# Graph attention over sorted edges: V products of three tiles in sixteen on POOL, K times Q sums of two on ACT, and masked maxima in place of a second pair of scans

## What is computed

```python
q = (x @ Wq + bq).reshape(n, H, DK)      # H = 8, DK = 64
k = (x @ Wk + bk).reshape(n, H, DK)
v = (x @ Wv + bv).reshape(n, H, DK)
logits = jnp.einsum('ehd,ehd->eh', q[rows] * scale, k[cols]) + att_bias
row_max = jax.ops.segment_max(logits, rows, num_segments=n)
p = jnp.exp(logits - row_max[rows])
denom = jax.ops.segment_sum(p, rows, num_segments=n)
att = p / denom[rows]
y = jax.ops.segment_sum(att[:, :, None] * v[cols], rows, num_segments=n)
out = y.reshape(n, H * DK) @ Wo + bo
```

## Time and profile before

| | |
|---|---|
| median of 3 runs | 3250.69 us (3249.51 to 3252.86) |
| profiled execution, its own time | 3252.61 us |
| span of the profile | 3250.8 us |
| busy: PE, DVE, ACT, POOL | 2883.9, 2864.1, 2188.3, 2211.0 us |
| granted TensorE clock, mean over the span | 0.94 |
| HBM read, written | 550.28 MB, 61.49 MB |

### The profile page before, as it was taken

How to read it: one execution, slowest core, us unless ns; L and a number is a source line. 1 busy time by engine, 2 the same in 40 slices (tenths; PEclk the granted TensorE clock), 3 DMA queues, 4 the chain that set the end, 5 groups by cost and what they waited for, 6 DMA issues and landing times.

```text
span 3250.8 us, 62874 instructions
## 1 busy us (share of the span) xinstructions
PE 2883.9 (89%) x11814; PEld 1680.8 (52%) x11939; DVE 2864.1 (88%) x20476; ACT 2188.3 (67%) x7706; POOL 2211.0 (68%) x2512
## 2 busy tenths in 40 slices
PE   4899888888888278999999999999999999989998
PEld 3555554445555135555555555555555555554444
DVE  8997777777777378999999999999999999998887
ACT  8332222222222048999999999999999999974444
POOL 0477777777777756777878778777878787851121
PEclk6798899888888689999999999999999999999999
DMA  6343333333333487888888888888888888841222
GB/s 188 84 136 105 107 111 107 113 107 107 106 104 93 163 307 251 262 262 259 259 261 263 260 259 265 259 264 259 264 260 260 260 263 259 259 140 61 83 79 71
DMA packets 259303, 615.95 MB, mean 189 GB/s; under 512 B 69771, under 2 KB 80343, under 8 KB 258658
## 3 DMA queue, kind: packets, MB, share of 16 engines
q0 software_dynamic: 144832, 443.72, 43.5%
q1 hardware_dynamic: 110434, 160.86, 16.5%
q10 hardware_dynamic: 3648, 7.34, 0.6%
HBM read 550.28 MB, written 61.49 MB: 188 GB/s over the span
## 4 chain that ended last, share of the span: by engine, by line
DVE 46%; POOL 23%; issue 14%; PE 12%; DMA 2%; DVEq 1%; ACT 1%; SPq 0%; POOLq 0%
DVE big L1339 25%; POOL rec_scratch L667 23%; DVE big L1449 12%; PE banks L2000 5%; PE banks L2065 2%; DVE big L1057 1%; DVEq L1449 1%; PE banks L1926 1%; PE banks L1979 1%; DMA big<-q_scratch 1%; DVE big L1434 1%; PE banks L1988 1%; DVE small L1401 1%; DMA big<-kv_scratch,small 1%; PE banks L2068 1%
## 5 line engine op out<-in xcount | busy, mean ns | idle before, releaser
L863 ACT ACTIVATE big<-big,small 128x65 f32<-128x65 f32 x6564 | 1605.1, 344 | 4.8
L688 POOL DMA_INDIRECT big<-kv_scratch,small x832 | 844.2, 1015 | 346.4 <-DVE big L1339 182.6
L1339 DVE SCALAR_TENSOR_TENSOR big<-banks,big 128x64 f32<-128x64 f32 x6656 | 1027.5, 213 | 32.6 <-DMA big<-kv_scratch,small 17.5
L667 POOL DMA_INDIRECT rec_scratch<-big,small x782 | 773.3, 989 | 323.4 <-issue 237.7
L1926 PE MATMUL banks<-big,small 128*128 x1664 | 889.7, 616 | 73.2 <-DVE big L1339 56.5
L1979 PE MATMUL banks<-big,small 128*128 128x260 f32 x3328 | 882.2, 388 | 45.6 <-POOL small L696 21.4
L1979 PEld LDWEIGHTS banks<-big,small 128*128 128x128 f32 x3328 | 615.0, 190 | 452.9 <-issue 271.9
L1817 PE MATMUL banks<-big 128*128 128x512 f32 (+1 forms) x1176 | 604.1, 662 | 34.8 <-DVE big L1047 34.8
L1449 DVE SCALAR_TENSOR_TENSOR big<-big,loS,banks 128x520 f32 x832 | 618.6, 744 | 6.3 <-PE banks L1979 4.2
L696 POOL TENSOR_SCALAR small<-iotaF,small 128x128 f32<-128x128 f32 x832 | 527.2, 634 | 60.5 <-PE banks L1979 34.8
L1339 DVE DVE_READ_ACCUMULATOR big<-banks,big 128x1 f32 x6656 | 513.5, 77 | 0.1
(11 more groups left out here) (273 smaller groups left out, 2639.7 us busy)
## 6 DMA issues: line engine op xcount, KB each, us to landing
rowR<-lo_rows SPq DMA_DIRECT2D x97, 256.0 KB
big<-src_rows SPq DMA_DIRECT2D x97, 256.0 KB, 3.6
big<-in_x_dram SPq DMA_DIRECT2D x96, 256.0 KB, 4.0
big<-kv_scratch,small POOLq DMA_INDIRECT x832, 5.3
rec_scratch<-big,small POOLq DMA_INDIRECT x782
kv_scratch<-big SPq DMA_DIRECT2D x48, 260.0 KB
q_scratch<-big SPq DMA_DIRECT2D x48, 256.0 KB
kv_scratch<-big SPq DMA_DIRECT2D x48, 256.0 KB
```

What stands on the lines that cost most here:

```text
L667: e.indirect_dma_start(recd, bass.IndirectOffsetOnAxis(ap=ridx[:, c % 4, j:j + 1], axis=0), rec[:, 8 * c + j, :], None).then_inc(s_sc[c % ...
L688: e.indirect_dma_start(KV[:, vat(t):vat(t) + YW + D], None, KVd, bass.IndirectOffsetOnAxis(ap=recB[b_ % 4][:, t % 16, 9:10].bitcast(i32), ...
L863: ins = e.activation(heads(Vr(t), h, h + 1), heads(Vr(t), h, h + 1), ACT.Copy, scale=ph[:, h:h + 1])
L1339: ins = e.scalar_tensor_tensor(k_, QB[t % 2][:, 64 * h:64 * h + 64], 1.0, k_, ALU.mult, ALU.mult, accum_out=Lr[t // 16 % 2][:, t % 16, h:h ...
```

## The change

Three parts, all in the attention stage.

1. `on_pool`: in each block the tiles t with t modulo 16 in (3, 8, 13) have V multiplied by p on POOL (`pvp`, one TENSOR_TENSOR of 128x520 with p broadcast along 65) instead of by 8 instructions on ACT. `pvp(s - 21)` stands on POOL behind `one_hot` in step s, so in steps r = 8, 13 and 2.
2. `summed`: the tiles with t modulo 16 in (4, 10), except in the last blocks, have K times Q as one DVE TENSOR_TENSOR of 128x512 in the first half of the step, and the sums over 64 by 8 ACTIVATEs with an accumulated sum on ACT (`sums`), two steps later and ahead of that step's `pva`. `gather` and `lb` wait for these sums.
3. `first_max` and `last_max`: the second pair of scans becomes two SCALAR_TENSOR_TENSORs on the result of the first pair, max(D2, mask + carried value), with masks that mark the edges of the tile's first and of its last source. The flags' row grows from 128 to 384 values for this, their buffers move to half of `rowR`, and the rows for the one-hots are loaded by half blocks. `scale_parts` becomes one instruction, with one more ACTIVATE on ACT (`p_less`) to take off 1.

The diff, cut to what the text speaks of:

```diff
-        QW = ((0, 8), (8, 16), (16, 24), (24, 28), (28, 33), (33, 40), (40, 49))
+        QW = ((0, 8), (8, 16), (16, 24), (24, 27), (27, 33), (33, 40), (40, 49))
...
-        sfr = [lc(130, bf16) for _ in range(2)]
+        sfr = [rowR[:, 1, 384 * i:384 * i + 384] for i in range(2)]
...
+        summed = [t % 16 in (4, 10) and t < LAST - 16 for t in range(T)]
+        sum_at = [sum(summed[:t + 1]) for t in range(T)]
+        s_sum, sum_base = s_ab, 2 * NCH
+        on_pool = [t % 16 in (3, 8, 13) and t < LAST for t in range(T)]
+        pvp_at = [sum(on_pool[:t + 1]) for t in range(T)]
+        s_pvp, pvp_base = s_hist, NCH
...
                 q.wait_ge(s_rd, k + 1)
+                if k >= 0:
+                    q.wait_ge(s_sum, sum_base + sum_at[k])
                 q.wait_ge(s_yt, v + 1)
...
+            def pvp(t):
+
+                v = Vr(t).rearrange("p (h d) -> p h d", d=65)
+                q.wait_ge(s_kv[t % 8], 16 * (t // 8 + 1))
+                q.wait_ge(s_ex, t // 16 + 1)
+                e.tensor_tensor(v, v, pB[t // 16 % 2][:, t % 16, :].rearrange("p (h a) -> p h a", a=1).broadcast_to([128, 8, 65]), ALU.mult).then_inc(s_pvp, 1)
...
                 if s - DEL - 2 >= 0:
                     one_hot(s - DEL - 2)
+                if 0 <= s - DEL + 2 < T and on_pool[s - DEL + 2]:
+                    pvp(s - DEL + 2)
...
+            def sums(t):
+
+                q.wait_ge(s_rd, t + 1)
+                q.wait_ge(s_x2, t // 16 - 1)
+                for h in range(8):
+                    k_ = Kr(t)[:, 64 * h:64 * h + 64]
+                    ins = e.activation(k_, k_, ACT.Copy, accum_out=Lr[t // 16 % 2][:, t % 16, h:h + 1])
+                ins.then_inc(s_sum, 1)
...
-                if s >= DEL:
+                if 2 <= s < T + 2 and summed[s - 2]:
+                    sums(s - 2)
+                if s >= DEL and not on_pool[s - DEL]:
                     pva(s - DEL)
                 if r_ == 5 and 0 <= b_ < NB:
                     p_fac(b_)
+                    p_less(b_)
                 if r_ == 6 and 0 <= b_ < NB:
                     p_exp(b_)
...
+                if summed[t]:
+                    if not half:
+                        e.tensor_tensor(Kr(t), QB[t % 2], Kr(t), ALU.mult).then_inc(s_rd, 1)
+                    return
                 for h in range(4 * half, 4 * half + 4):
...
-            def fwd2(b_):
+            def first_max(b_):
 
                 q.wait_ge(s_car, 2 * b_ + 2)
-                e.tensor_tensor_scan(F2, sfr[b_ % 2][:, 0:128], XP, Car[:, 1:2], ALU.add, ALU.max).then_inc(s_f2, 1)
-
-            def back2(b_):
+                q.wait_ge(s_d1, b_ + 1)
+                e.scalar_tensor_tensor(D2[b_ % 2], sfr[b_ % 2][:, 128:256], Car[:, 1:2], D2[b_ % 2], ALU.add, ALU.max).then_inc(s_f2, 1)
+
+            def last_max(b_):
 
                 q.wait_ge(s_f2, b_ + 1)
-                q.wait_ge(s_dt, b_ - 1)
-                e.tensor_tensor_scan(D2[b_ % 2][:, ::-1], sfr[b_ % 2][:, 1:129][:, ::-1], F2[:, ::-1], Car[:, 0:1], ALU.add, ALU.max).then_inc(s_m2, 1)
+                e.scalar_tensor_tensor(D2[b_ % 2], sfr[b_ % 2][:, 256:384], Car[:, 0:1], D2[b_ % 2], ALU.add, ALU.max).then_inc(s_m2, 1)
...
-                e.tensor_tensor(Aoh[0:8, :], iotaF[0:8, :], llb[0:8, max(b_ - 1, 0):max(b_ - 1, 0) + 1].broadcast_to([8, 128]), ALU.is_equal).then_inc(s_bd, 1)
-                e.scalar_tensor_tensor(Bd[0:8, :], ident[0:8, 0:8], fac[0:8, 0:1], nI[0:8, :], ALU.mult, ALU.add).then_inc(s_bd, 1)
+                e.scalar_tensor_tensor(Aoh[0:8, :], iotaF[0:8, :], llb[0:8, max(b_ - 1, 0):max(b_ - 1, 0) + 1], fac[0:8, 0:1].broadcast_to([8, 128]),
+                                       ALU.is_equal, ALU.mult).then_inc(s_bd, 1)
```

More of the change, by code:

```diff
@@ L549, in _ @@
             q.wait_ge(s_c5, 3)
-            rows5(0)
-            rows5(1)
-            q.wait_ge(s_idb, 3)
+            rows5(2)
+            rows5(3)
+            q.wait_ge(s_c5, 2)
             flags(0)
@@ L578, in _ @@
                     recs(b_)
-                q.wait_ge(s_rm, 4 * b_ - 4)
-                rows5(b_)
+                if b_ >= 5:
+                    q.wait_ge(s_ya, 16 * (b_ - 4))
+                    keeps(b_ - 1)
+                q.wait_ge(s_rm, 4 * b_ - 2)
+                rows5(2 * b_)
                 if b_ == 2:
@@ L851, in p_fac, with p_less @@
                 q.wait_ge(s_dd, b_ + 1)
-                q.wait_ge(s_bd, 2 * b_)
+                q.wait_ge(s_bd, b_)
                 e.activation(fac[0:8, 0:1], fac[0:8, 1:2], ACT.Exp, scale=-1.0).then_inc(s_fac, 1)
+            def p_less(b_):
+                q.wait_ge(s_fac, 2 * b_ + 1)
+                e.activation(fac[0:8, 0:1], fac[0:8, 0:1], ACT.Copy, bias=-1.0).then_inc(s_fac, 1)
+            def sums(t):
[5 more added lines that the diff above has]
+                ins.then_inc(s_sum, 1)
             def heads(v, h0, h1_):
@@ L1309, in one_hot_rows @@
                 e.memset(sfb[0:n, c, 0:1], 1.0).then_inc(s_v, 1)
-                nv += 2
+                for m in range(2):
+                    e.tensor_tensor(sfb[0:n, c, 128 + 128 * m:256 + 128 * m], lo_, ends2[0:n, c, m:m + 1].broadcast_to([n, 128]), ALU.is_equal).then_inc(s_v, 1)
+                nv += 4
                 e.tensor_tensor(rows3[0:n, c, 2, :], sqf[c % 2][0:n, :], rows3[0:n, c, 1, :], ALU.subtract).then_inc(s_v, 1)
@@ L1325, in _ @@
             first_oh(1)
-            for k in range(2):
-                e.memset(sfr[k][:, 128:129], 0.0).then_inc(s_idb, 1)
             win = wins(e, "dw")
@@ L1535, in _ @@
                 if at == 4:
-                    fwd2(b_)
+                    first_max(b_)
                 if at == 6:
@@ L1553, in _ @@
                 if at == 4:
-                    back2(b_)
+                    last_max(b_)
                 if s < T:
@@ L1932, in rows_oh @@
                 q.wait_ge(s_oh, k)
-                q.wait_ge(s_r[b_ % 2], 16 * (b_ // 2 + 1))
+                h = k // 2
+                q.wait_ge(s_r[h % 2], 16 * (h // 2))
                 q.wait_ge(s_c5, 3)
-                e.matmul(OHB, coef[:, :], row5[:, b_ % 2, 512 * (k % 4):512 * (k % 4) + 512], start=True, stop=True).then_inc(s_rm, 1)
+                e.matmul(OHB, coef[:, :], row5[:, h % 2, 512 * (k % 2):512 * (k % 2) + 512], start=True, stop=True).then_inc(s_rm, 1)
             def x2(b_):
@@ L1964, in scale1 @@
             def scale1(b_):
-                q.wait_ge(s_bd, 2 * b_ + 2)
+                q.wait_ge(s_bd, b_ + 1)
                 q.wait_ge(s_ex, b_ + 1)
                 q.wait_ge(s_sca, b_ - 1)
-                e.matmul(S1, Aoh[0:8, :], Bd[0:8, :], start=True, stop=True).then_inc(s_s1, 1)
+                e.matmul(S1, Aoh[0:8, :], ident[0:8, 0:8], start=True, stop=True).then_inc(s_s1, 1)
             def yt(t):
-                q.wait_ge(s_pva, t + 1)
+                q.wait_ge(s_pva, t + 1 - pvp_at[t])
                 q.wait_ge(s_pvv, t - LAST + 1)
+                if pvp_at[t]:
+                    q.wait_ge(s_pvp, pvp_base + pvp_at[t])
                 q.wait_ge(s_oh2, t + 1)
```

44 lines of the change are left out of this document (23 added, 21 removed).

## The result

The kernel with the change takes 3492.31 us (median of 4 runs, 3488.00 to 3495.82) against 3250.28 us before: a ratio of 1.0745, 95% interval 1.0731 to 1.0758. The forecast was 3373 us with a range up to 3460. The direction was right, and POOL's wait for the exponential came at the place predicted, though 5 us long where 2 stood; the size was twice the forecast's.

What follows compares the result with a forecast made beforehand. DVE and ACT were taken to bound the attention stage together at 33.1 us a block; the change's loop of waits makes it 35.5. 3252.6 + 117 + 5 = 3374.6, less 1.9 to the median: 3373 us, range 3265 to 3460.

Steps and rivals of the forecast that it cites:

- The loop: Attention stage: POOL's tile 3 product awaits the exponential, through gathers, DVE and ACT; 35.5 us a block against 33.1, 117 us.
- ACT: signal 0.1, 8 sums 2.3: Loop's ACT part after the product of tile 20: signal, sums, last `pva` 1.97, exponential 0.25; from 30.95 to 35.55 us.
- So I count nothing: POOL's product can hold up DVE's small instructions for its whole 1.3 us; round the loop this was counted as zero.
- the landing decides: Loop at tile 16: DVE gets there before gather 16 lands, 5.3 us after its start, at 21.07 us.
- SP and PE. ... Both at nothing: One-hot row loads, longer flags and PE's unchanged instructions: hidden by room, zero cost; PE has 5% idle under 33.1 us.
- POOL's part: Loop from the exponential's end: signal, product, gap, gathers 9 to 16; gather 16 starts at 15.77 us.
- The start: Before the attention stage: larger flag store, a later Q window, added comparisons and copies; 5 us, between 0 and 15.
- The product on POOL: One `pvp` of 128x520 on POOL, priced from L703: 1.29 us, 1.33 with the gap to the one before.
- A sum: One accumulating ACTIVATE of 128x64 on ACT: 0.29 us, the middle of 0.16 to 0.42.
- rival 2: Port lock on top: tile 13's `pvp` hits `back1` or `first_max`; 31 us more, 3404 us, at worst 3435; chance 0.12.
- DVE near 88%: Sign expected in the changed profile: DVE busy near 31.4 / 35.5 = 88%.
- Rival 3: DVE becomes the bound at 31.4 us a block, the exponential there before POOL asks: faster, 3173 us; chance 0.08.

Runs made afterwards that it cites:

- e3: The change without sums on ACT (all K times Q sums back on DVE), POOL's products kept: 3640.19 us, 1.0445 of the kernel before on the same chip.
- e5: The change with ACT's sums at tiles (5, 10) instead of (4, 10): 3668.31 us, 1.0507 of the kernel before on the same chip.
- f4: The same kernel as e3, run again beside f1: 3635.24 us, 1.0452 of the kernel before on the same chip.
- h1: The change with ACT's sums one step behind DVE instead of two: 3766.99 us, 1.0758 of the kernel before on the same chip.
- f1: The change with POOL's products at tiles (6, 10, 14) and no sums on ACT: 3472.24 us, 0.9985 of the kernel before on the same chip.
- h2: The change with POOL's products at tiles (6, 10, 14) and sums one step behind DVE: 3531.55 us, 1.0070 of the kernel before on the same chip.

## Why the prediction was right in direction and wrong in size

- **The loop: right.** POOL's wait at r = 8, ended by the exponential and once a block, is there; moving the products behind it takes it and 168 us away.
- **The first step that failed is "ACT: signal 0.1, 8 sums 2.3".** It takes ACT to be free when the product of tile 20 is done. In fact the sums start 1.72 us behind it (+1.6): the copy of the one-hot rows, a product of V, `p_fac` and `p_less` stand ahead of them, and PE's rows come only 0.76 us before that product starts. The prediction put ACT's whole work under the loop's length and did not follow its order at this place. This is read from the trace; no run moves the copy or that product out of the way.
- **The second is "So I count nothing" for POOL's product beside DVE, with "the landing decides".** At `lb` the product of tile 13 holds DVE up. In the ten rounds at full clock tile 16 starts at 21.80, where a landing of 5.3 us behind gather 16 gives 20.6 (+1.2). Without the hold-up, 0.19 us after the start of `lb` as in the round shown, it would by my estimate have been 20.5 to 21.3.
- **The third is "SP and PE. ... Both at nothing".** The clock was 1.00 before and is 0.96 in 1500 to 2900 us: some 8% of the time at half speed, 3.0 us a block. The mean round, 37.9 us, is 0.5 longer than the ten rounds at full clock. So the clock explains about 0.5 us of a block, some 25 us of the 235, and not the rest. That is read from rounds of one trace: no run changes the clock alone. The runs with the products at their early place have 0.93 to 0.97 (the change, e3, e5, f4, h1), those without 1.00.
- **The sum again**, for a round at full clock: 35.55 forecast, -0.4 for POOL's part, +1.2 for tile 16, -0.1 for tiles 16 to 20, +1.6 ahead of the sums, -0.4 for the sums and what follows: 37.4; with the clock 37.9. The 0.1 for a signal stood in no row; on POOL it was 0.14 and 0.44 us.
- **The start: 5 us forecast**, 3.3 measured at the first scan, 6.9 at the first rescaling (1243.4 to 1250.3). The 5.3 us behind the last scan were not in the sum. In total the start was near the forecast.
- **Prices.** The product on POOL: 1.06 us, forecast 1.29 (the bound from L703 lay above it, and the sum had no lower end). A sum: 0.24 us from one ACTIVATE to the next, forecast 0.29; eight take 2.0 us, of which the read of the sum, an instruction of its own of 186 ns, is the half that was unknown. The Trainium skill (ScalarE: Activation LUTs, What ACT_TABLE_LOAD costs) gives 186 ns + 0.833 ns per column, 239 ns for 64; the trace agrees, with a median of 239. It has no price for the read, and so its 1.2 us for eight was too low.
- **Both were cheaper than forecast, and the time was longer.** Errors of the prices and signals were worth 0.9 us a block downwards, what was left out 3.3 upwards. The range's upper end, 3460, was made of prices and of rival 2, and had nothing for ACT's order or PE.
- **DVE near 88%**, one of the signs named, came out at 86%, but by two errors: DVE's block has 32.7 us of work and not 31.4, in part because `lb` is held up, and the block is 37.9 and not 35.5.
- **Rival 2, the shared port:** right in kind, but at `lb` (L1390) and not at `back1` or `first_max`, beside the product of tile 13: median 486 ns, up to 1908, where L1347 had 283. It does not come on top of every round, as the rival has it: the rounds with an `lb` of over 1 us are nearly all among the shortest, 37.4. It fixes the start of tile 16 where nothing else makes DVE late. What a round without it would take, no run shows.
- **Rival 3, faster, DVE at 31.4:** with the wait out of the way (f1) DVE is the bound, as the rival says, at 32.8 without the first blocks. It has the sums' 1.1 us to do itself, and the maxima with the scaling gave 0.3 to 0.4 and not 0.6, and 31.4 + 1.1 + 0.2 or 0.3 is 32.7 or 32.8. With late products and one-step sums (h2) it takes 33.9: the sums' waits eat what they free.
